# Moving one projection ahead of the first transposed maxima, and two batches' transposes behind it

## The reference

```
qkv = x @ w_qkv + b_qkv                       # x: layer-normed tokens, [4, 256, 192]
attn = softmax(einsum('bhqd,bhkd->bhqk', q, k) * 16**-0.5)
out = einsum('bhqk,bhkd->bhqd', attn, v)
t = t + out @ w_proj + b_proj
```

## Time and profile before

| what | value |
|---|---|
| timed runs | 242.6, 245.27, 245.29 us |
| median | 245.27 us |
| the profiled execution's own time | 243.01 us |
| its span | 241.2 us |
| mean granted TensorE clock over the span | 0.981 of full |
| PE busy | 224.1 us (93%) |
| DVE busy | 150.5 us (62%) |
| ACT busy | 113.3 us (47%) |
| POOL busy | 76.9 us (32%) |

### The profile page before, as it was taken

The page is one execution under the profiler, slowest core; times in us unless marked ns, Lnnn a source line. Parts: engine busy times, 40 slices in busy tenths (PEclk is TensorE's granted clock), DMA queues, the critical chain, the costliest instruction groups (busy, mean ns, idle before and its releaser), DMA issues.

```text
span 241.2 us, 5781 instructions
## 1 busy us (share of the span) xinstructions
PE 224.1 (93%) x1968; PEld 146.3 (61%) x1968; DVE 150.5 (62%) x353; ACT 113.3 (47%) x199; POOL 76.9 (32%) x119
## 2 busy tenths in 40 slices
PE   2999999799999999999889999999999999998972
PEld 2988876555667667686565755555556565553371
DVE  0126777626888887978667866666665666552383
ACT  0345037224544443515536265666665656564203
POOL 7003007000000180265410335665656566531000
PEclk9999999959999999999999999999999999999998
DMA  7961399803685988710830011111111211211524
GB/s 192 234 155 23 88 309 259 247 9 77 208 257 111 279 228 236 214 38 0 281 83 0 22 44 37 50 49 49 52 46 49 60 49 43 53 25 35 170 95 130
DMA packets 28099, 27.67 MB, mean 115 GB/s; under 512 B 7788, under 2 KB 26796, under 8 KB 28076
## 3 DMA queue, kind: packets, MB, share of 16 engines
q1 hardware_dynamic: 23372, 21.40, 32.5%
q0 software_dynamic: 2304, 4.72, 6.8%
q10 hardware_dynamic: 2400, 1.26, 2.1%
HBM read 22.49 MB, written 3.44 MB: 107 GB/s over the span
## 4 chain that ended last, share of the span: by engine, by line
PE 85%; DVE 5%; DMA 3%; issue 3%; ACT 2%; ACTq 0%; DVEq 0%
PE grid L1526 11%; PE bank L1552 9%; PE grid L1293 9%; PE grid L1533 7%; PE bank L1311 4%; PE bank L1542 4%; PE bank L1158 3%; PE bank L1328 3%; PE grid L1110 3%; PE bank L1264 3%; PE bank L1216 3%; PE grid L1264 2%; PE grid L1425 2%; PE bank L1278 2%; PE bank L1219 2%
## 5 line engine op out<-in xcount | busy, mean ns | idle before, releaser
L1044 DVE COPY main<-main 128x1152 f32 x41 | 31.6, 783 | 15.6 <-issue 13.8
L748 ACT ACTIVATE main<-down_all 128x576 f32 x42 | 28.6, 684 | 27.1 <-PE bank L1552 26.0
L717 ACT ACTIVATE main<-grid 128x1024 f32<-128x1024 f32 x24 | 24.5, 1024 | 30.0 <-PE grid L1293 30.0
L582 POOL DMA_INDIRECT main<-xhat_rows,main x21 | 26.5, 1261 | 24.5 <-DVE main L1006 11.7
L1526 PE MATMUL grid<-main 128*64 128x384 f32 x160 | 29.8, 488 | 0.3 <-DVE main L1028 0.3
L590 POOL DMA_INDIRECT pair_rows<-main x19 | 20.4, 1072 | 25.6 <-DVE main L1034 25.6
L1264 PE MATMUL grid<-main 32*128 32x256 f32 x132 | 28.5, 419 | 0.0
L1293 PE MATMUL grid<-main 32*128 32x256 f32 x192 | 26.8, 408 | 0.8 <-ACT main L717 0.6
L858 DVE TENSOR_REDUCE main<-grid 128x2 f32<-128x512 f32 x33 | 21.8, 685 | 5.6 <-PE grid L1264 4.8
L1552 PEld LDWEIGHTS bank<-main 128*64 128x64 f32 x228 | 16.2, 136 | 12.3 <-ACT main L748 9.6
L1552 PE MATMUL bank<-main 128*64 128x192 f32 x228 | 22.7, 333 | 0.2
(11 more groups left out here) (200 smaller groups left out, 402.7 us busy)
## 6 DMA issues: line engine op xcount, KB each, us to landing
down_all<-wd SPq DMA_DIRECT2D x4, 1152.0 KB, 9.2
main<-wg SPq DMA_DIRECT2D x4, 576.0 KB, 4.6
main<-wu SPq DMA_DIRECT2D x4, 576.0 KB, 6.2
main<-wg SPq DMA_DIRECT2D x4, 288.0 KB, 7.0
main<-wu SPq DMA_DIRECT2D x4, 288.0 KB, 8.2
main<-main SPq DMA_DIRECT2D x8, 128.0 KB, 2.5
main<-x SPq DMA_DIRECT2D x1, 768.0 KB, 5.9
main<-wg SPq DMA_DIRECT2D x2, 384.0 KB, 4.0
```

Of the source, the lines that this page charges most:

```text
L582: pool.indirect_dma_start(xg[:, t % 2, :], None, xhat_rows, bass.IndirectOffsetOnAxis(ap=slot_token[:, t:t + 1].bitcast(U32), axis=0)).the ...
L717: act.activation(probs[:, quad % 2, 2 * (n % 2):2 * (n % 2) + 2, :, :].rearrange("p h k n -> p h (k n)"), grid[:, score_banks(n), :], ACT. ...
L748: act.activation(w_dn[:, p, h, :], dn_e(expert(t, h)), ACT.Copy).then_inc(S["w_dn_ready"], 1)
L1044: vec.tensor_copy(w_gu[:, p, h, :], gu_e(expert(t, h))).then_inc(S["w_gu_ready"], 1)
```

## The change

It changes the order of existing work on PE and ACT, with nothing computed in another way.

- On PE the transposes xhat_T(2) and xhat_T(3) move from between the maxima of units 0 and 1 into slot 0, behind the maxima of unit 3. So unit 1's maxima stand right behind unit 0's.
- project_pair(1) (quads 3 and 4) moves from slot 0 to behind unit 1's maxima, ahead of maxima_rows(0).
- On ACT dense_rows(1) moves from behind exponential 0 to behind values(0), and the copies xT_rows(2), xT_rows(3) from there to behind exponential 0.
- project_pair(p) with p over 0 waits for `first_ready` and `wait_evicted`, and only from p = 2 on for all four xT copies. xhat_T(2) waits for four evicted quads (`dense_ready` 4) in place of two, and no longer for `img_ready`.

```diff
-DENSE_AT = (None, 0, 1, 3, 7, 13)
+DENSE_AT = (None, None, 1, 3, 7, 13)
...
             first_queries_keys()
             dense_rows(0)
             values(0)
-            for b in range(2, B):
-                xT_rows(b)
+            dense_rows(1)
             for n in range(SPAN):
...
+                if n == 0:
+                    for c in range(2, B):
+                        xT_rows(c)
                 if n in DENSE_AT:
...
                 if b == 2:
-                    pe.wait_ge(S["img_ready"], 4)
                     pe.wait_ge(S["first_ready"], 2)
-                    pe.wait_ge(S["dense_ready"], 2)
+                    pe.wait_ge(S["dense_ready"], 4)
...
                 if p:
+                    pe.wait_ge(S["first_ready"], 2)
+                    wait_evicted()
+                if p >= 2:
                     pe.wait_ge(S["xT_ready"], B)
-                    wait_evicted()
...
             for qh in range(2):
                 pair_for_max(0, qh)
-            for b in range(2, B):
-                xhat_T(b)
             for qh in range(2):
                 pair_for_max(1, qh)
+            project_pair(1)
             maxima_rows(0)
...
                 for part in range(2 if n + LEAD < SPAN else 0):
                     pair_for_max(n + LEAD, part)
+                if n == 0:
+                    for c in range(2, B):
+                        xhat_T(c)
                 if n % 2 and n + 1 < SPAN:
                     maxima_rows((n + 1) // 2)
```

## The result

| | median us | lowest | highest | executions |
|---|---|---|---|---|
| before | 243.54 | 242.3 | 246.63 | 22 |
| changed | 243.97 | 238.65 | 246.11 | 22 |

The ratio of the changed kernel to the kernel before is 0.9855, with a 95% interval of 0.9821 to 0.9889. It compares only the executions within 1.5% of each kernel's fastest, 9 of the changed kernel's 22 and 17 of the 22 before, so it favours the changed kernel, whose median did not move; the means over all 22 are 242.73 against 244.11 us, 0.6% apart. So two numbers describe the change: its fastest execution is 3.6 us faster (238.65 against 242.3), and half of its executions gain nothing.

What follows compares the result with a forecast made beforehand. The prediction took PE, nearly always busy, as the bound, with 1.38 us idle and 6.8 us at half clock to gain from: 243.01 - 0.44 - 3.41 = 239.2 us, range for 8 in 10 238.0 to 244.6.

Steps and rivals of the forecast that it cites:

- Step 1: Unit 1's maxima directly behind unit 0's: DVE reduces without a gap, done at 44.79 instead of 45.52 us.
- Steps 2 and 3: project_pair(1) behind unit 1's maxima; maxima_rows(0) then waits for ACT's evictions: PE idle 0.95 instead of 1.38 us, -0.4 us.
- Step 4: Transposes and ACT's xT copies in slot 0: copies cost nothing, at most 1.09 us once; project_pair(2) at 51.5 us.
- Step 5: spread_rows(1) on SP issued about 46 instead of 53.99 us: costs nothing, room grows from 1.1 to over 5 us.
- Step 6: The 6.8 us half-clock stretch from about 47.8 us disappears, clock stays full: -3.4 us; forecast given 0.60.
- Rival A: Clock falls as before around the thin 32-row work; only the idle saving counts: 242.6 us, chance 0.25.
- Rival B: With transposes in slot 0, the half-clock stretch lasts half as long again, +1.7 us: 244.3 us, chance 0.10.
- Rival C: Evictions ahead of maxima_rows(0) come 0.43 us later, idle time is 1.38 us again, clock falls: 243.0 us, chance 0.05.

Runs made afterwards that it cites:

- e8: Changed kernel, first transposed maxima waiting only for pair 0's evictions, and copies of quads 1 and 2 ahead of the first down-weight load: median 240.17 us, ratio 0.9826.
- e10: Changed kernel, first transposed maxima waiting only for pair 0's evictions, loads in their old order: median 241.29 us, ratio 0.9887.
- e11: Kernel before with only project_pair(1) and its evictions moved, first transposed maxima waiting for pair 0 only, copies ahead of the first down-weight load: median 239.05 us, ratio 0.9843.
- e1: The changed kernel run again, unaltered: 238.79 to 245.67 us, median 242.13, ratio 0.9823; its profiled execution took 239.15 us.
- e5: Kernel before with only the transposes and ACT's copies of batches 2 and 3 moved to slot 0, ahead of project_pair(1): median 247.19 us, ratio 1.0121.
- e3: Kernel before with SP's second expert load held back until the copies of quads 1 and 2 have landed: median 245.18 us, ratio 0.9998.
- e4: Kernel before with three extra 128-row matmuls, results never read, in PE's idle time ahead of maxima_rows(0): median 240.96 us against 244.79, ratio 0.9852.
- e7: Changed kernel with SP's first down-weight load moved behind the copies of quads 1 and 2: median 242.93 us, ratio 0.9802; profiled execution 244.54 us.

## Why the prediction was right or wrong, step by step

*Step 1, unit 1's maxima behind unit 0's.* Right: DVE reduces without a gap, 2.49 us for all four.

*Steps 2 and 3, the projection and its evictions.* Right, to 0.1 us: ACT releases `maxima_rows(0)`, with 1.03 us of idle time where 0.95 was worked out. e8, e10 and e11 showed that this wait can be dropped, since bank 5 belongs to pair 0 only. The prediction took it as given.

*Step 4, transposes and copies in slot 0.* Right in e1's profile: no other wait of PE up to 60 us, and project_pair(2) in the chain at 51.67 where 51.5 was forecast. e5 shows how much the cover was worth: with the projection right behind the transposes, the same copies cost 0.73 us.

*Step 5, the DMA.* Here something was missed. Only pair 1's copies were priced. Pair 0's, read by unit 2's maxima right behind `maxima_rows(0)`, had about half a microsecond of room in the profile of before (landed by 45.4, needed at 45.9), and with the loads in their old order they land anywhere from 44.8 to 47.3, behind the load issued at 32 to 33.4 us. The change neither makes nor mends this: e3, e4 and e5, all built on the kernel before, wait 1.14 to 2.52 us for them.

*Step 6, the clock, -3.4 us.* The mechanism was right and its certainty was not. Where the clock stays full, the time is 239.15 us against a forecast of 239.2, and e4 shows the cause directly. But only 10 of 28 executions have under 6 us at half clock, where the forecast gave the full clock six chances in ten. The step argued from two idle stretches, of 1.06 and 1.07 us, that no fall had followed, seen in one execution, in places with other work. The one near 220 us bears this out: all 14 profiles have it, at 1.02 to 1.08 us, and none has a fall behind it. Behind the one near 115 us the clock does fall in 8 of 14 profiles, 7.8 to 10.5 us later and within 2.7 us of a wait of only 0.69 us, which the other 6 have too. e7 against e1 shows that one and the same 1.03 us, with the same work of PE on both sides, is followed by a fall in one execution and not in another. The idle time moves the odds of the fall; what decides in a single execution stays open, and one trace is one draw.

*Rival A* (the clock falls all the same) was given 0.25, and e7's profile is its case: 6.8 us, though its 244.5 us also hold the 6.8 us in the routing. *Rival B* forecast half clock for half as long again and 244.3 us; the first profile has 10.2 us and 244.5. Its time was hit, its cause was not: in e7 the transposes stand in slot 0 too and the stretch is 6.8 us, while e3 has 10.2 us with no transposes there. What the long ones share is a wait for the copies of 1.5 us or more: e3, e5 and the first profile, against 6.8 us in e7 without one. *Rival C* did not occur.

The Trainium skill's line on transposes ("TensorE: Matmul & The Clock Gate", section "Part 4: PE-mode transpose") is neither borne out nor refuted: e7's stretch is no longer than that of before, though the transposes took a projection's place in it.

*The number.* Against the median the forecast of 239.2 was 4.8 us too low, and its 2.5% came out as 1.4% (the ratio) or nothing (the median). The range held because it took in A and B, not because the forecast's clock was there; that the median lies inside it is no support for step 6. Where the text set the 245.3 us of two timed runs aside, it had a sign of this: 2.3 us between executions of one program would be, at the changed kernel's 0.50 us for each, the cost of 4.6 us more at half clock. And the prediction counted on one place with a low clock, since its one trace had only one.

## What to carry to other kernels

Fill PE's short waits ahead of thin matmuls (those on 32 rows), with useful work if there is some. When a few microseconds at half clock hang on such a wait, only a share of the executions pays them, so look at the mean granted clock of many executions before one profile's story is taken for the kernel's, and look in several profiles for other places where the clock falls. When a step is moved to the front, list every producer of what comes next, DMAs too, with the room each has left and how far its landing time spreads, and check whether a general "wait for all evicted" now covers more than the bank it guards.

## What the runs showed of the hardware

One program's executions differ by up to 7.5 us (238.65 to 246.11) almost only through TensorE's clock: 0.50 us of time for each microsecond at 1.2 GHz (28 executions of the changed kernel, correlation 0.97). The stretches at half clock that ended while PE had work lasted from 3.4 to 13.7 us in these profiles. A wait of 0.69 us in the routing was followed within 2.7 us by a fall in 8 of 14 profiles, one of 1.02 to 1.08 us between 128-row matmuls near 220 us in none. A 1152 KB load issued at 32 to 33.4 us landed 11.1 to 13.8 us later, and two copies of 128 KB issued 7.4 to 9.9 us behind it took 2.5 to 6.0 us; with that load behind them they took 2.4 to 3.3 us in all five profiles.
